# Attention on one Trainium2 core: ScalarE copies the transposed probabilities before it takes the exponential of a later tile

## The reference

```python
# L0 attention, once: 16 heads in 4 groups, 1024 positions
scores = jnp.einsum('bhqd,bhkd->bhqk', qw, kw) * scale + bias   # bias: -inf on and above the diagonal
m = jnp.max(scores, axis=-1, keepdims=True)
e = jnp.exp(scores - m)
p = e / jnp.sum(e, axis=-1, keepdims=True)
out = jnp.einsum('bhqk,bhkd->bhqd', p, vs)
...
# L2 attention, twice: 32 heads in 8 groups of 4, head width 64, rotary q and k
scores = jnp.einsum('bqhd,bkhd->bhqk', q, k) / np.float32(np.sqrt(HEAD_DIM))
scores = jnp.where(causal[None, None], scores, jnp.float32(-1e+30))
attn = jax.nn.softmax(scores, -1)
o = jnp.einsum('bhqk,bkhd->bqhd', attn, v).reshape(B, S, NHEADS * HEAD_DIM)
x = x + o @ wo
```

## Time and profile before

| what | value |
|---|---|
| median of 3 runs | 3843.64 us (3839.55 to 3846.38) |
| profiled execution: its own time | 3848.8 us |
| profiled execution: span of the core | 3846.9 us |
| mean granted TensorE clock | 0.944 of full |
| busy: PE, PEld | 3325.0 us, 2631.2 us |
| busy: DVE, ACT, POOL | 2473.0 us, 1949.4 us, 1668.8 us |
| ACT L1213 exponentials, 640 | 475.5 us |
| ACT L1229 copies, 960 | 436.1 us |
| PE L1147 and L1151 scores, 960 each | 413.5 us, 394.3 us |
| PE L1163 transposes, 2880 | 441.6 us |
| PE L1183 values, 1440 | 443.6 us |

### The profile page before, as it was taken

The page is one execution under the profiler, slowest core; times in us unless marked ns, Lnnn a source line. Parts: engine busy times, 40 slices in busy tenths (PEclk is TensorE's granted clock), DMA queues, the critical chain, the costliest instruction groups (busy, mean ns, idle before and its releaser), DMA issues. The chain is left out here.

```text
span 3846.9 us, 58222 instructions
## 1 busy us (share of the span) xinstructions
PE 3325.0 (86%) x18336; PEld 2631.2 (68%) x18336; DVE 2473.0 (64%) x4854; ACT 1949.4 (51%) x3927; POOL 1668.8 (43%) x1269
## 2 busy tenths in 40 slices
PE   5798798479898989988995999788889987998979
PEld 4566586148566666667883899556666666887868
DVE  4787544955577878875446656477777876445554
ACT  3787433333476767754333322266666774334333
POOL 1666211832466667742211544176666662221111
PEclk8999799889999999999996999799999999999989
DMA  2000232323101111003320000110111102332222
GB/s 79 22 30 3 77 108 64 133 91 115 60 25 31 30 27 32 20 4 120 114 73 16 1 1 1 42 35 24 25 28 27 30 12 82 115 109 83 73 94 74
DMA packets 81189, 204.66 MB, mean 53 GB/s; under 512 B 16923, under 2 KB 20123, under 8 KB 80662
## 3 DMA queue, kind: packets, MB, share of 16 engines
q1 hardware_dynamic: 80774, 201.26, 16.8%
q10 hardware_dynamic: 144, 0.07, 0.0%
HBM read 171.39 MB, written 4.69 MB: 46 GB/s over the span
## 5 line engine op out<-in xcount | busy, mean ns | idle before, releaser
L1246 POOL TENSOR_TENSOR probs<-probs,row_inverse 128x640 f32<-128x640 f32 (+7 forms) x640 | 737.4, 1158 | 538.5 <-DVE row_inverse L1272 528.1
L548 PE MATMUL psUp<-xnT_part,weights_part 128*128 128x512 f32 x3456 | 843.3, 394 | 2.8 <-DVE hidden L689 1.8
L548 PEld LDWEIGHTS psUp<-xnT_part,weights_part 128*128 128x128 f32 x3456 | 636.4, 190 | 126.1 <-issue 2.4
L525 POOL TENSOR_TENSOR weights_part<-weights,weights_part 128x768 fp32r<-128x768 f32 x136 | 251.2, 1851 | 1029.3 <-ACT weights_part L598 1029.3
L1260 DVE TENSOR_REDUCE neg_max<-psS 128x1 f32<-128x640 f32 (+7 forms) x640 | 476.8, 745 | 149.1 <-PE psS L1151 147.9
L1287 DVE TENSOR_TENSOR probsT_part<-psT,probsT_part 128x512 fp32r<-128x512 f32 (+1 forms) x960 | 502.3, 551 | 89.9 <-ACT probsT_part L1229 78.7
L1229 ACT ACTIVATE probsT_part<-psT 128x512 fp32r<-128x512 f32 (+1 forms) x960 | 436.1, 490 | 219.9 <-PE psT L1163 216.7
L1213 ACT ACTIVATE probs<-psS,neg_max 128x640 f32<-128x640 f32 (+7 forms) x640 | 475.5, 743 | 96.9 <-DVE neg_max L1260 83.2
L1147 PE MATMUL psS<-k_part,q_parts 128*128 128x512 f32 (+1 forms) x960 | 413.5, 431 | 114.1 <-ACT probs L1213 73.9
L559 PEld LDWEIGHTS psDown<-weights_part,hidden_part 128*128 128x128 f32 x3456 | 458.2, 194 | 56.0 <-issue 23.3
L559 PE MATMUL psDown<-weights_part,hidden_part 128*128 128x256 f32 x3456 | 468.0, 286 | 31.2 <-DVE hidden_part L709 31.2
(11 more groups left out here) (310 smaller groups left out, 4771.6 us busy)
## 6 DMA issues: line engine op xcount, KB each, us to landing
gates<-gate_rows SPq DMA_DIRECT2D x136, 512.0 KB, 4.0
weights<-in_l_ffn SPq DMA_DIRECT2D x148, 384.0 KB, 4.4
qk_swapped<-qk_raw SPq DMA_DIRECT2D x384, 64.0 KB, 2.0
bc_broadcast<-bc_rows SPq DMA_DIRECT2D x32, 512.0 KB, 4.6
w_group<-in_l_wgroup SPq DMA_DIRECT2D x16, 384.0 KB, 3.2
q_whole<-q_steps SPq DMA_DIRECT2D x32, 128.0 KB
w_o_group<-in_l_wo SPq DMA_DIRECT2D x16, 256.0 KB, 3.2
rope<-in_l_rope SPq DMA_DIRECT2D x2, 1024.0 KB, 5.5
```

The source lines that it names most:

```text
L525: nc.gpsimd.tensor_tensor(w[1][:, j, :], wt[:, j, :], w[0][:, j, :].bitcast(F32), ALU.subtract).then_inc(w_split, 1)
L548: last = nc.tensor.matmul(psU[:, u % 2, g, :], wp[:, j, g * D + k * P:g * D + (k + 1) * P], xp[:, k, cols(half)], start=n == 0, stop=n == ...
L1246: self.nc.gpsimd.tensor_tensor(self.p[:, n % 4, 0:w], self.p[:, n % 4, 0:w], self.rinv[:, at:at + 1].to_broadcast([P, w]), ALU.mult).then_ ...
```

## The change

ScalarE's `exp(g, s + 7, last)` moves from ahead of the copies of unit s+4 to behind them. No other engine's instructions change.

```diff
@@ -1218,7 +1218,6 @@
                 act.wait_ge(self.valued, NT * g + s // 4 + 1)
                 act.wait_ge(self.kept, NT * g + s // 4 + 1)
                 nc.scalar.activation(self.shift[:], self.psO[64:64 + self.dv, :], ACT.Copy).then_inc(self.shifted, 1)
-            exp(g, s + 7, last)
             n = s + 4
             if self.exists(n, last):
                 for j, c in enumerate(self.chunks(n)):
@@ -1227,6 +1226,7 @@
                         act.wait_ge(self.valued, NT * g + n // 4 - 1)
                     out, in_ = self.piece(0, n, j, c)
                     nc.scalar.activation(out, in_, ACT.Copy).then_inc(self.first[self.bank(c)], 1)
+            exp(g, s + 7, last)
             self.hooks.act_step(act, g, s, last)
         self.run(act, groups, lambda: exp(0, 0, False), step)
```

## The result

The change takes 4196.64 us (median of 4, 4188.74 to 4200.63) against 3843.2 before: 353 us more, a ratio of 1.0916, 95% interval [1.0898, 1.0933]. The forecast was 4120 in a range of 4030 to 4260: slower, by the mechanism named, with 77 us of size missing. The profiled execution took 4188.74 us with a span of 4186.7, the shortest of the four; the one before took 3848.8, 5 us above its median. So the two profiles are only 340 us apart, 13 less than the medians.

What follows compares the result with a forecast made beforehand. PE's own work bounded attention; the change would close a ring of 2.76 us a step. L0 +92, L2 stages +164 and other waits +20 gave +276 us, 4120 us on the median; range 4030 to 4260.

Steps and rivals of the forecast that it cites:

- the ring: Attention loop, closing once each step: scores, transposes, copies, exponential, next scores; 2.76 us a step, chance 0.80 at full clock.
- The pieces outside: Stages outside attention: they should keep their times to 1 us.
- The four terms: One lap: scores to transposes 0.65 us, transposes to first copy 0.67, copies 0.56, exponential to next scores 0.88.
- L0, +92 us: First-layer attention: 2.76 against 2.04 us a step, 0.72 us more in each of 128 steps.
- the falling clock: Rival: PE's gaps in attention lower its granted clock, giving 4212 to 4304 us or beyond; chance 0.15.
- the forecast's own sign: Granted clock in attention below 0.9 would make the forecast wrong and point to the clock's fall.
- the ring at full clock: All attention stages: the loop decides steps with the clock unlowered; 4120 us, own range 4025 to 4203, chance 0.80.
- L2, +82 us each: Each of two third-layer attention stages: 2.91 against 2.59 us a step, 0.32 us more in 256 steps.
- What the ring doesn't cover, +20 us: PE's waits for GpSimd's scaled probabilities and a group's last-step output: 1 us a group, 20 groups.
- Absorption by ScalarE's idle time: Rival: ScalarE absorbs the delay and earlier copies pay, 3820 us, chance 0.03; no change, 3844 us, 0.02.

Runs made afterwards that it cites:

- turn_first: The change, with PE also issuing the transposes of tile s+4 ahead of the scores of tile s+8: 4005.67 us, ratio 1.0418.
- turn_b: The kernel before, ScalarE's order untouched, with PE's transposes issued ahead of its scores: 3987.61 us, ratio 1.0364.
- pieces_after: The change, with every ScalarE copy of transposed blocks cut into copies of one block: 4347.4 us, ratio 1.1313.
- filler_l0: The change, with six small bfloat16 filler matmuls a step on PE in the L0 attention alone: 4172.36 us, ratio 1.0851.
- open_old: The change, with ScalarE's order of before in the opening steps (s below 0) of each attention stage: 4165.54 us, ratio 1.0832.
- pieces_before: The kernel before, with every ScalarE copy of transposed blocks cut into copies of one block: 3870.61 us, ratio 1.0065.

## Why the prediction was right, and where it was short

**The bound and the ring.** Right. PE's wait for the exponential comes in 112 of 128 steps of L0; the exponential no longer waits for the maxima. The pieces outside moved by up to 6.8 us where 1 us had been said, but by -4 in all. That it is a ring and not ScalarE's order shows from two sides: PE's order takes back 191 us (turn_first), and the ScalarE orders differ by 18 us once PE's is turned (turn_b). That its terms add one behind another shows in pieces_after: 151 us against 24.5.

**The four terms.** Right: 0.43, 0.79, 0.75 and 0.73 in the lap above, where the forecast's rule for a step of these widths gives 0.44, 0.73, 0.76 and 0.72. At full clock L0 runs at 2.77 us a step against 2.76.

**L0, +92 us.** Undersized: the stretch alone grew by 109.8, and the forecast's 0.72 x 124 is 89. The missing 20 us are the clock. The forecast held the falling clock for a rival with 0.15; it came in part, together with the ring. By the forecast's own sign, a clock below 0.9 in attention, L0 belongs to that rival; yet its stretch lost 91 us to the ring (343.7 at full clock against 253.1) and 19 to the clock, so the sign was too coarse. The stretch stayed at 0.89 instead of 0.99, and without that (filler_l0) it is 343.7 us. The step that failed is "the ring at full clock", which relied on the scan stage's 60 us at a busy share of 0.57 and clock 1.00.

**L2, +82 us each.** Undersized by about 20 us each; the stretches grew by 100.8 and 100.2, where 0.32 x 252 is 81. One group at full clock, 1685.96 to 1781.24, takes 95.3 us and not 93. Most of that, by the steps of this group, is a term wrongly placed. Weight loads of three steps:

```profile
1688.04 0.41 PEld L1496 LDWEIGHTS psT<-xnT,w_group 128*128 128x128 f32 x2
...
1689.55 0.19 PEld L1147 LDWEIGHTS psS<-k_part,q_parts 128*128 128x128 f32 x1 [0.24 <-issue]
...
1690.72 0.46 PEld L1163 LDWEIGHTS psT<-ident,probs 128*128 128x128 f32 x4
1692.99 0.19 PEld L1147 LDWEIGHTS psS<-k_part,q_parts 128*128 128x128 f32 x1 [1.08 <-ACT probs L1213]
...
1693.83 0.46 PEld L1163 LDWEIGHTS psT<-ident,probs 128*128 128x128 f32 x4
```

Behind a projection the scores take 1.17 us (1689.55 to 1690.72) to reach the transposes, against 0.84 (1692.99 to 1693.83). The forecast counted this among PE's work in the projection's step, where it competes with the ring, and put it at 0.2 us. It lies in the next step, on the ring: 0.33 x 6, 2 us a group, 32 us in 16 groups. An average group takes 95.8 us (754.1 / 252 x 32), 2.8 more than the 93 of the forecast; the other 0.8 us was not taken apart, and no run changed this term alone.

**The openings.** The forecast priced 128 and 256 steps at the mean gain and so gave the first steps of a stage 0.72 and 0.32 us each. They have no values and no jobs to hide a ring behind, and in L0 the clock of the opening was 0.65 (0.84 in open_old, 0.92 before). They cost 33 us, of which open_old gave back 27; the forecast had some 5 of them in its steps (4 at 0.72, 8 at 0.32).

**What the ring doesn't cover, +20 us.** Too much. GpSimd's wait left PE's list; longer steps did give it its time. That two errors had opposite signs is luck. Between the two profiles the account is: L0 +20, L2 +40, openings +27, this term -20, the pieces outside -4, together 63 of the 64 us between 340 and 276. The other 13 of the 77 are the distance of the profiled executions from their medians.

**The rivals.** The clock rival came in part, 24 us in L0 by filler_l0. The Trainium skill's page TensorE: Matmul & The Clock Gate, section "A second HAM failure mode: psum-queue depth-cycling", says that short idles between groups of matmuls can swing the clock. L0's trace agrees, with a mean of 0.89 and waits in 112 of 128 steps, and the scan stage's row misled; the L2 stretches stayed at 0.97 and 0.98. Absorption by ScalarE's idle time didn't come; what its idle time can absorb shows in pieces_before, where the copies grew by 120 us (436.1 to 556.3) and the kernel by 24.5.

## What to carry to other kernels

When engines with in-order queues work on a pipeline, write out for each wait how many steps lie between producer and consumer, and look for loops that close within one step; a swap of two instructions on an engine with half its time idle can take such a loop from two steps to one. Then the step costs the sum of the loop's terms, which can be read from the kernel before, start to start. Check every such loop through every pair of engines, not those of the busiest alone, and count the openings and the clock of the longer, emptier step apart.

## What the hardware showed that wasn't expected

The granted clock of L0 fell to a mean of 0.89 though PE's waits for the exponential there are only 0.9 us on average and 1.8 us at most. And a low stretch need not look empty: in the opening of L0, 8.4 us at the 1.2 GHz level are 0.94 full of PE work, of which each piece takes longer there, while later laps, with a share of 0.69, ran at the 2.4 GHz level:

```profile
131.50:139.90 8.40, 7.90 (x25) 5.59 (x25) 3.59 (x8) 2.75 (x6) 2.08 (x2) 0.50 0.01 2
256.50:266.30 9.80, 6.81 (x34) 4.36 (x32) 5.97 (x13) 5.52 (x12) 4.19 (x3) 1.00 0.00 0
```

A lap of the same widths took 4.32 us in the first (135.58 to 139.90) and 3.10 behind it (139.90 to 143.00): from the scores' start to the first copy it was 2.78 and then 1.57 us, and ScalarE's part stayed (1.54 and 1.53). And idle work that PE does in its own gap paid: 720 more matmuls in L0's stretch (2007 instead of 1287) made it 19 us shorter, at a granted clock of 1.00 instead of 0.89.
